# Router work of four batches moved between the items of the top-64 attention

## Chip, cores and metric

One core of one Trainium2 chip runs the kernel. The metric is the device time of one execution in microseconds; lower is better. TensorE does matmuls and transposes, VectorE (DVE) reductions, selections and small tables, ScalarE (ACT) activations and copies out of PSUM, GpSimd (POOL) elementwise work on SBUF and the indirect transfers, SyncE (SP) issues the other transfers.

## What is computed

Four blocks of gated attention and feed-forward over `x` (8 batches, 256 rows, 256 features). The change touches the third block: the top-64 attention and the router of the mixture of experts behind it.

```python
x = x + tanh(g_xattn[2]) * _L2_xattn_ref(_layernorm(x), ctx, ctx, mask, 64, ...)   # 16 heads, 77 keys, best 64 of them
x = x + tanh(g_ffn[2]) * _L2_ffn_ref(_layernorm(x), router_w, w1, w2)

# _L2_ffn_ref: 8 experts, each row goes to the best 2
logits = x_flat @ router_w.T
probs = softmax(logits); top_v, top_i = top_k(probs, 2)
...                       # rows get a place in their experts' lists, in order, up to a capacity
h = gelu(einsum('ech,ehf->ecf', expert_in, w1)); y = einsum('ecf,efh->ech', h, w2)
```

## The kernel before

All activations stay in SBUF as `x[128, 16, 256]`: batch b is rows 2b and 2b + 1 of the middle axis. Each engine runs its own instruction list, written out by hand; the order in the code is the order on the engine. Engines meet in counting semaphores: `then_inc` on the producer and `wait_ge` on the consumer, `past(n)` standing for the n-th count of a phase. A wait blocks everything behind it on that engine.

**The top-64 attention** works on B = 8 batches in PAIRS = 4 pairs, and on each pair in ITEMS = 8 items (4 head groups by 2 batches); N4 = 32 items in all, item i in buffer i % 2. All engines loop over k and handle, in iteration k, items near k:
- TensorE: `top_scores(k + 2)`; a part of the output projection `top_final` if k is in `top_parts`; `top_probs(k - 2)`, eight transposes of probabilities into `ps[2]`; `top_values(k - 2)`; turn and queries of the next pair.
- ScalarE: `top_abs(k - 1)`, `top_out(k - 3)` for every other couple of items, `top_scores(k + 1)` (copy out of PSUM), `top_exp(k - 1)` in two halves of four activations, between them turn and queries of the next pair, `top_turned_probs(k - 2)`, `top_norm` of the next pair.
- GpSimd: `top_shift(k - 1)` with its pads, `top_norm(k - 2)`, `top_mask(k + 1)`, `top_bias` at j = k % 8 in (4, 5), `top_scale` and `top_keys` of the next pair.
- VectorE: `drop_least(k)`, which removes the 13 least of 77 scores of each row and head (a min, then twice max8 and match_replace over 8 rows of 77), then `top_stats`, or `top_residual`, which adds a finished part of the projection to `x`.

`top_parts` sets when the projection of pair q is made: for q = 0, 1, 2 at k = 8q + 10, 14, 15, 16, a quarter each. The rows of pair 0 are complete behind iteration 16, those of pair 1 behind 24. The last pair's projection stands behind the last values: `top_final(3, m)` for m = 0 to 3, m = 0, 1 reading `oT[0]` (which is `xkeep` rows 8 to 11) and m = 2, 3 reading `oT[1]` (rows 12 to 15). `top_last(p)` adds it to `x`.

**The router** works by batch: `l5_stats` (VectorE: mean and variance of two rows), `l5_scale` (GpSimd: the reciprocal root and the shift), `l5_norm` (ScalarE, writes `xkeep`), `l5_flip` (TensorE: four transposes into bank 2), `l5_turned` (ScalarE: copy into `xnT`), `l5_logits` (TensorE: eight matmuls of eight columns into bank 3), and on VectorE `l5_take`, `l5_choose`, `l5_keep`: copy the logits, the best two and their numbers. Behind the last batch VectorE builds the routing tables (cumulative sums, one-hot tiles), GpSimd gathers rows by them, and 39 tiles of 128 rows go through the experts.

**Transfers around it.** SyncE has issued the first weights of all experts and the second of expert 0. It then waits for `done[4]` (all rows of the attention), issues the second weights of experts 1 to 4 (1 MB each), stores of the eight normalised batches (256 KB each, each waiting for its `l5_norm`), the second weights of experts 5 to 7, and, when all stores have landed, the last block's weights.

Of the kernel before, what the change touches and what calls it, by code (L numbers as in the profile page):

```python
# [14 lines left out]
P = 128  # L15
# [11 lines left out]
E = 8  # L27
# [12 lines left out]
def build(nc, a, out, phases=8):  # L40
# [10 lines left out]
    with ctx:  # L51
# [219 lines left out]
        NORMS = (0, 4, 5)  # L271
# [13 lines left out]
        stat = shared("stat", {0: B, 4: TT, 5: B})  # L285
# [3 lines left out]
        xts = shared("xts", {n: B for n in NORMS})  # L289
        done = shared("done", {0: B, 3: TT, 4: TT})  # L290
# [96 lines left out]

        def top_kb(q, p):

            return kb[p] if q else kb_first[p]  # L390
# [11 lines left out]
        def _(sp):  # L402
# [28 lines left out]
            if phases >= 6:  # L431
# [10 lines left out]
                for e in range(E):  # L442
                    first(e)
                second(0)
                sp.wait_ge(done[4].sem, done[4].past(TT))
                for e in range(1, 5):
                    second(e)
                for b in range(B):
                    sp.wait_ge(keep_s.sem, keep_s.past(b + 1))
                    sp.dma_start(xs_d[b * S:(b + 1) * S, :].rearrange("(t p) d -> p t d", p=P),  # L450
                                 xkeep[:, TB * b:TB * b + TB, :]).then_inc(s_kd, 16)
# [25 lines left out]
        def _(gp):  # L477
# [89 lines left out]
            if phases >= 4:  # L567
# [101 lines left out]
                for k in range(N4 + 2):  # L669
# [77 lines left out]
        def _(ac):  # L747
# [205 lines left out]
            if phases >= 4:  # L953
# [12 lines left out]
                def l5_norm(b):  # L966
                    p = b % 2
                    ac.wait_ge(rstd[5].sem, rstd[5].past(b + 1))
                    if b >= B // 2:
                        ac.wait_ge(f_p[4].sem, f_p[4].past(TT))  # L970
                    post_norm(xkeep[:, TB * b:TB * b + TB, :], rows2(b), rs_b[p], nm_b[p]).then_inc(keep_s.sem, 1)

                def l5_turned(b):
# [3 lines left out]
                    copy(xnT[b % 2][:, :, :].rearrange("p c s -> p (c s)"), bank(2)).then_inc(xts[5].sem, 1)  # L977

# [9 lines left out]
                def top_queries(q, p):  # L988
# [104 lines left out]
                for k in range(N4 + 3):  # L1093
# [20 lines left out]
                    if k == N4:  # L1114
                        l5_norm(0)
            if phases >= 5:
                for b in range(1, B):
# [124 lines left out]
        def _(ve):  # L1242
# [237 lines left out]
            if phases >= 4:  # L1480
# [66 lines left out]
                def l5_take(b):  # L1547
                    ve.wait_ge(lg_p.sem, lg_p.past(b + 1))
                    nc.vector.tensor_copy(lg[b % 2][:, :, :], bank(3)[:, 0:TB * E].rearrange("p (t e) -> p t e", t=TB)
# [13 lines left out]
                def l5_keep(b):  # L1563
# [3 lines left out]
                    nc.vector.tensor_copy(topi[:, TB * b:TB * b + TB, :], ix[p][:, :, 0:2]).then_inc(rt_c.sem, 1)  # L1567

# [1056 lines left out]
```

## Time and profile before

| what | us |
| --- | --- |
| median of 3 runs | 994.3 |
| lowest and highest | 991.7, 994.53 |
| profiled execution, its own time | 991.3 |
| its span in the profile | 989.4 |
| items 0 to 31 of the top-64 attention end (last match_replace) | 517.2 |
| last logits of the router taken | 550.9 |
| first expert weights copied | 573.7 |

The last three lines are positions in the span. Line numbers (L...) are those of the kernel before. In a row of the timeline the numbers are start and duration in us, then engine, line, operation, output and inputs, and the idle time of the engine just before with what ended it. An entry `x8` merges eight instructions.

### The profile page before, as it was taken

To read this page: it belongs to the slowest core of one execution; us is meant where nothing else is said; L and a number is where in the kernel's file an instruction comes from. 1 tells how busy PE (TensorE), PEld (TensorE's weight loads), DVE (VectorE), ACT (ScalarE), POOL (GpSimd) and SP (SyncE) were. 2 spreads that over 40 slices of the span, in tenths; PEclk is the share of its full clock that TensorE was granted. 3 is DMA by queue.
4 is the path that set the end of the run, shared out by engine and by line. 5 is a ranking of instruction groups with operands and counts; after the bars stand their busy time and mean duration, and the time that the engine had idled before them with its cause. 6 is when DMAs were issued, how large, how long until landed. Compare 5 with 4: busy or idle time off the path is not lost.

```text
span 989.4 us, 17402 instructions
## 1 busy us (share of the span) xinstructions
PE 812.4 (82%) x5192; PEld 659.3 (67%) x5198; DVE 646.4 (65%) x2713; ACT 516.3 (52%) x1252; POOL 490.3 (50%) x712
## 2 busy tenths in 40 slices
PE   5899999996764767767568479999999999847986
PEld 4577767873452445545347369999999999736775
DVE  3877766889978999999994742222222222367875
ACT  3777755689964889788776012121121211225652
POOL 2566535676635777777565132222323222138993
PEclk9899999999996767879877579999999999968999
DMA  9100001000000090000003911111101111050001
GB/s 292 35 1 2 2 2 43 1 2 0 2 1 1 31 354 1 1 2 1 1 1 103 338 39 38 33 44 32 44 32 37 39 33 33 21 171 0 24 22 42
DMA packets 32934, 47.02 MB, mean 48 GB/s; under 512 B 3158, under 2 KB 27582, under 8 KB 32843
## 3 DMA queue, kind: packets, MB, share of 16 engines
q1 hardware_dynamic: 29099, 35.69, 10.6%
q0 software_dynamic: 3744, 10.23, 3.3%
q8 instruction: 44, 0.72, 0.3%
q14 instruction: 47, 0.39, 0.1%
HBM read 36.60 MB, written 9.31 MB: 46 GB/s over the span
## 4 chain that ended last, share of the span: by engine, by line
PE 52%; DVE 29%; POOL 8%; ACT 4%; issue 4%; DMA 2%; SPq 0%; DVEq 0%; POOLq 0%; ACTq 0%
PE ps L2425 14%; PE ps L2436 14%; DVE experts L1516 5%; DVE experts L1526 5%; DVE m8b L1521 3%; PE ps L1991 3%; DVE m L1511 3%; PE ps L2014 3%; PE ps L1978 2%; DVE mx L1506 2%; PE ps L2001 2%; PE ps L1938 2%; DVE sm L1444 1%; PE ps L2112 1%; DMA x<-in_x 1%
## 5 line engine op out<-in xcount | busy, mean ns | idle before, releaser
L2425 PE MATMUL ps<-xnT,ptall 128*128 128x128 f32 x1248 | 147.3, 277 | 0.0
L2425 PEld LDWEIGHTS ps<-xnT,ptall 128*128 128x128 f32 x1248 | 144.1, 194 | 0.1
L2436 PE MATMUL ps<-experts,wk 128*128 x624 | 141.2, 379 | 1.3 <-ACT xkeep L754 1.3
L1743 DVE COPY ptall<-experts 128x512 f32 x156 | 60.0, 427 | 120.9 <-PE ps L2425 115.1
L699 POOL DMA_INDIRECT xn<-expert_in,rown x39 | 38.1, 976 | 179.2 <-PE ps L2413 164.8
L2436 PEld LDWEIGHTS ps<-experts,wk 128*128 128x128 f32 x624 | 115.6, 190 | 15.8 <-issue 1.7
L1131 ACT ACTIVATE wk<-ps 128x1024 f32<-128x1024 f32 x39 | 39.9, 1024 | 127.4 <-PE ps L2425 127.4
L1028 ACT ACTIVATE experts<-experts,mcol 128x77 f32<-128x77 f32 x256 | 87.8, 350 | 0.1
L754 ACT ACTIVATE xkeep<-ps 128x256 f32<-128x256 f32 x87 | 33.2, 381 | 100.8 <-PE ps L2436 97.1
L1762 DVE COPY xnT<-ps 128x256 f32<-128x256 f32 x39 | 16.5, 424 | 79.0 <-PE ps L2413 79.0
L2280 PE MATMUL ps<-ptall,experts 77*32 77x256 f32 x256 | 25.3, 474 | 51.7 <-ACT ptall L1036 51.7
L523 POOL TENSOR_TENSOR experts<-experts,rden 128x616 f32<-128x616 f32 x32 | 38.8, 1216 | 47.8 <-DVE rden L1301 47.8
L707 POOL DMA_INDIRECT token_out<-xkeep,dest x39 | 38.5, 987 | 44.2 <-ACT xkeep L754 34.1
L613 POOL TENSOR_TENSOR experts<-experts,mx 128x616 f32<-128x616 f32 x32 | 39.1, 1223 | 38.9 <-DVE experts L1526 38.9
L606 POOL TENSOR_TENSOR experts<-experts 128x616 f32<-128x616 f32 x32 | 44.4, 1388 | 26.6 <-ACT experts L1006 26.6
L1516 DVE MATCH_REPLACE8 experts<-m,experts 128x80 f32<-128x80 f32 x256 | 54.7, 233 | 0.0
L1526 DVE MATCH_REPLACE8 experts<-m8b,experts 128x80 f32<-128x80 f32 x256 | 54.7, 233 | 0.0
L2269 PEld LDWEIGHTS ps<-ident,experts 128*77 128x77 f32 x256 | 37.8, 185 | 22.0 <-POOL experts L639 14.2
L2269 PE MATMUL ps<-ident,experts 128*77 128x128 f32 x256 | 43.7, 327 | 10.6 <-POOL experts L639 7.0
L754 ACT ACTIVATE experts<-ps 128x512 f32<-128x512 f32 (+2 forms) x56 | 39.5, 712 | 24.2 <-PE ps L1938 19.0
L754 ACT ACTIVATE ptall<-ps 77x512 f32<-77x512 f32 (+1 forms) x80 | 41.0, 545 | 21.2 <-PE ps L1991 18.2
L1028 ACT ACTIVATION_READ_ACCUMULATOR experts<-experts,mcol 128x1 f32 x256 | 49.3, 193 | 0.0
(303 smaller groups left out, 2049.0 us busy)
## 6 DMA issues: line engine op xcount, KB each, us to landing
experts<-in_ew SPq DMA_DIRECT2D x16, 1024.0 KB, 11.5
experts<-token_out SPq DMA_DIRECT2D x16, 256.0 KB, 5.2
x<-in_x SPq DMA_DIRECT2D x1, 2048.0 KB, 11.0
xkeep<-in_bw SPq DMA_DIRECT2D x2, 1024.0 KB, 7.1
expert_in<-xkeep SPq DMA_DIRECT2D x8, 256.0 KB, 6.5
out<-x SPq DMA_DIRECT2D x8, 256.0 KB, 2.1
xn<-expert_in,rown POOLq DMA_INDIRECT x39, 2.8
token_out<-xkeep,dest POOLq DMA_INDIRECT x39, 2.4
```

Of the source, the lines that this page charges most:

```text
L523: nc.gpsimd.tensor_tensor(flat(soft[j]), flat(soft[j]), rden[i % 2][:, :].unsqueeze(2) .broadcast_to([P, 8, KEYS]), ALU.mult).then_inc(sm_ ...
L606: nc.gpsimd.tensor_tensor(dv, dv, mrow[:, b * KEYS:(b + 1) * KEYS].unsqueeze(1) .broadcast_to([P, TB * HG, KEYS]), ALU.add).then_inc(mk_s, 1)
L613: nc.gpsimd.tensor_tensor(dv, dv, mx[u][:, :].unsqueeze(2).broadcast_to([P, TB * HG, KEYS]), ALU.subtract).then_inc(sc_d.sem, 1)
L754: return nc.scalar.activation(dst, src, ACT.Copy)
L1028: ins = nc.scalar.activation(row, row, ACT.Exp, scale=mcol[:, b:b + 1], accum_out=ssum[u][:, j:j + 1])
L1131: nc.scalar.activation(hidT[j % 2].rearrange("p (v n) -> p v n", v=2), ps[j % 2][:, :, :], ACT.Gelu).then_inc(m_g.sem, 1)
L1516: ins = nc.vector.match_replace(d[j], m8[u][:, j, :], d[j], -BIG)
L1526: ins = nc.vector.match_replace(d[j], m8b[u][:, j, :], d[j], -BIG)
L1743: ins = nc.vector.tensor_copy(tilew[:, v, c, :], experts[:, bass.ds(e * EW + (c * FF + v * 512), 512)])
L2269: ins = nc.tensor.transpose(ps[2][0:KEYS, h // 2, at:at + P], pr[i % 2][:, t, h * KEYS:(h + 1) * KEYS], ident[:, :])
L2425: ins = nc.tensor.matmul(ps[j % 2][:, v, k * P:(k + 1) * P], tilew[:, v, c, k * P:(k + 1) * P], xTb[j % 3][:, c, :], start=c == 0, stop=c ...
L2436: ins = nc.tensor.matmul(bank(4)[:, 0:D], hidT[j % 2][:, k * P:(k + 1) * P], experts[:, bass.ds(e * EW + (E * EW + k * D), D)], start=k == ...
```

## The change

- **Norms and turns.** `l5_at = {16: 0, 20: 1, 24: 2, 28: 3}` puts the router's batches 0 to 3 into the attention loop. For k in it, `l5_stats` follows item k on VectorE; `l5_scale` follows in GpSimd's iteration k + 1 and `l5_norm` in ScalarE's; `l5_flip_half` (four transposes into the upper halves of banks 6 and 7) follows `top_probs` in TensorE's iteration k + 2; `l5_turned_half` (two copies of 128x256 into free halves of `wk[0]`) stands between the exponentials in ScalarE's iteration k + 3.
- **Logits.** `l5_logits_half` of batches 0, 1, 2 stands ahead of the scores of items 23, 27, 31, that of batch 3 in iteration 32; they go to columns 320 to 383 of bank 3. `top_queries(3, 0)` on ScalarE waits for the first of them, because the turned batch 0 lies in its output.
- **Choices.** `l5_pick` (take, keep of the batch before, choose) of batches 0 and 1 stands in VectorE's iteration 32, of 2 and 3 ahead of `top_last`.
- **Last pair's projection.** `top_final(3, 0)` stands ahead of the last values, `top_final(3, 1)` behind them, then 2 and 3. `l5_norm(4)` and `(5)` wait for the first two parts of it instead of all.
- **Behind.** Only batches 4 to 7 are left, with the functions of before.
- **Stores.** Those of batches 0 to 3 stand ahead of the wait for `done[4]`.
- **Semaphores.** `stat`, `rstd`, `xtp` and `xts` of the router become semaphores of their own.

```diff
-        stat = shared("stat", {0: B, 4: TT, 5: B})
+        stat = shared("stat", {0: B, 4: TT})
+        stat[5], rstd[5], xtp[5], xts[5] = (counted(n) for n in ("stat5", "rstd5", "xtp5", "xts5"))
+        l5_at = {16: 0, 20: 1, 24: 2, 28: 3}
+        l5_logit_at = {23: 0, 27: 1, 31: 2}
...
 SyncE
                 second(0)
+                for b in range(B // 2):
+                    stored(b)
                 sp.wait_ge(done[4].sem, done[4].past(TT))
                 for e in range(1, 5):
                     second(e)
-                for b in range(B):
+                for b in range(B // 2, B):
...
 GpSimd
+                    if k - 1 in l5_at:
+                        l5_scale(l5_at[k - 1])
                     if k == N4:
-                        l5_scale(0)
+                        l5_scale(B // 2)
...
 ScalarE
-                        ac.wait_ge(f_p[4].sem, f_p[4].past(TT))
+                        ac.wait_ge(f_p[4].sem, f_p[4].past(TT - 2 if b < B - 2 else TT))
+                def l5_turned_half(b, k):
+                    ac.wait_ge(xtp[5].sem, xtp[5].past(b + 1))
+                    ac.wait_ge(pv_p[4].sem, pv_p[4].past(k - 2))
+                    if b:
+                        ac.wait_ge(lg_p.sem, lg_p.past(b))
+                    for t in range(TB):
+                        ins = copy(xT5[b][:, t, :, :].rearrange("p c s -> p (c s)"), bank(6 + t)[:, S:2 * S])
+                    ins.then_inc(xts[5].sem, 1)
+                    elif q == 3 and p == 0:
+                        ac.wait_ge(lg_p.sem, lg_p.past(1))
+                    if k - 3 in l5_at:
+                        l5_turned_half(l5_at[k - 3], k)
                     if 1 <= k < N4 + 1:
                         top_exp(k - 1, 1)
                     if 2 <= k < N4 + 2:
                         top_turned_probs(k - 2)
+                    if k - 1 in l5_at:
+                        l5_norm(l5_at[k - 1])
...
 VectorE
+                def l5_pick(b):
+                    l5_take(b)
+                    if b:
+                        l5_keep(b - 1)
+                    l5_choose(b)
                     if k == N4:
-                        for b in range(2):
-                            l5_stats(b)
+                        l5_stats(B // 2)
...
+                    if k in l5_at:
+                        l5_stats(l5_at[k])
+                    if k == N4:
+                        for b in range(2):
+                            l5_pick(b)
-                for b in range(2, 5):
-                    l5_stats(b)
+                l5_stats(B // 2 + 1)
+                for b in range(2, B // 2):
+                    l5_pick(b)
                 for p in range(2):
                     top_last(p)
+                    l5_stats(B - 2 + p)
...
 TensorE
+                def l5_flip_half(b, k):
+                    pe.wait_ge(keep_s.sem, keep_s.past(b + 1))
+                    pe.wait_ge(oc_s, sum(i // 2 % 2 for i in range(k - 2)))
+                    for t in range(TB):
+                        for c in range(CH):
+                            ins = nc.tensor.transpose(bank(6 + t)[:, S + c * P:S + (c + 1) * P],
+                                                      xkeep[:, TB * b + t, c * P:(c + 1) * P], ident[:, :])
+                    ins.then_inc(xtp[5].sem, 1)
+                def l5_logits_half(b):
+                    pe.wait_ge(xts[5].sem, xts[5].past(b + 1))
+                    ...
+                            ins = nc.tensor.matmul(l5_cols(b)[:, t * E:(t + 1) * E], xT5[b][:, t, c, :], rwT[:, c, :],
+                                                   start=c == 0, stop=c == CH - 1)
+                    ins.then_inc(lg_p.sem, 1)
+                    if i in l5_logit_at:
+                        l5_logits_half(l5_logit_at[i])
...
+                    if k == N4:
+                        pe.wait_ge(sc_r[4].sem, sc_r[4].past(N4))
+                        pe.wait_ge(done[4].sem, done[4].past(top_parts[k - 2] + 1))
+                        l5_logits_half(B // 2 - 1)
                     if 2 <= k < N4 + 2:
                         top_probs(k - 2)
+                        if k - 2 in l5_at:
+                            l5_flip_half(l5_at[k - 2], k)
+                        if k - 3 in l5_at:
+                            pe.wait_ge(xts[5].sem, xts[5].past(l5_at[k - 3] + 1))
                         if k == N4 + 1:
-                            l5_flip(0)
+                            top_final(PAIRS - 1, 0, k)
                         top_values(k - 2)
                     if k >= N4 + 2:
-                        for m in range(2 * (k - N4 - 2), 2 * (k - N4 - 1)):
+                        for m in range(1, 2) if k == N4 + 2 else range(2, 4):
                             top_final(PAIRS - 1, m, k)
-                for b in range(1, B):
+                l5_flip(B // 2)
+                for b in range(B // 2 + 1, B):
                     l5_flip(b)
                     l5_logits(b - 1)
```

## Rows read from the trace of the kernel before

**Rows 1.** The page: VectorE's busy share in 40 slices of the span, tenths.
```profile
DVE  3877766889978999999994742222222222367875
```
**Rows 2.** Busy time by stretch: from:to, length, engines' busy us, clock, DMA share, GB/s.
```profile
411.50:517.20 105.70, 72.36 (x392) 49.48 (x392) 105.70 (x809) 85.49 (x321) 71.03 (x76) 0.80 0.00 1
497.50:504.00 6.50, 4.34 (x20) 2.52 (x20) 6.50 (x52) 5.20 (x21) 4.95 (x5) 0.74 0.00 1
510.80:517.20 6.40, 4.54 (x25) 3.47 (x24) 6.40 (x52) 5.20 (x19) 2.16 (x2) 0.59 0.00 0
517.20:535.30 18.10, 14.70 (x95) 11.85 (x95) 7.01 (x28) 10.41 (x30) 10.75 (x23) 0.72 0.00 1
535.30:551.10 15.80, 14.83 (x84) 14.00 (x83) 8.26 (x76) 8.51 (x17) 4.29 (x12) 0.65 0.98 317
551.10:573.70 22.60, 4.85 (x36) 3.25 (x36) 18.64 (x55) 0.22 (x1) 3.86 (x2) 0.50 0.77 261
```
**Rows 3.** The chain of waits in order of time, 517 to 552: start, length.
```profile
528.36 6.06 PE ps L2314 x32
...
549.04 1.86 PE ps L2299 x8
```
**Rows 4.** Timeline of VectorE: start and duration in us.
```profile
503.94 0.80 DVE L1506 TENSOR_REDUCE mx<-experts 128x8 f32<-128x616 f32 x1
...
517.68 0.71 DVE L1539 BATCH_NORM_STATS2 st_b<-x 128x6 f32<-128x256 f32 x2
...
518.53 0.72 DVE L1539 BATCH_NORM_STATS2 st_b<-x 128x6 f32<-128x256 f32 x2
```
**Rows 5.** Timeline of GpSimd, from k = 16 to the drain.
```profile
418.39 1.22 POOL L613 TENSOR_TENSOR experts<-experts,mx 128x616 f32<-128x616 f32 x1
...
500.59 1.28 POOL L606 TENSOR_TENSOR experts<-experts 128x616 f32<-128x616 f32 x1 [0.46 <-ACT experts L1006]
501.82 1.27 POOL L632 TENSOR_TENSOR x<-x,experts 128x512 f32<-128x512 f32 x1
...
519.84 0.23 POOL L590 TENSOR_SCALAR rs_b<-mv_b 128x2 f32<-128x2 f32 x1
...
520.96 0.50 POOL L595 TENSOR_SCALAR nm_b<-mv_b,rs_b 128x1 f32<-128x1 f32 x2
```
**Rows 6.** Who waited for whom, 411.5 to 517.2: total us, times, longest.
```profile
PE ps L2280 <- ACT ptall L1036: 26.3, 15, 3.3
```
**Rows 7.** Timeline of ScalarE.
```profile
503.13 1.01 ACT L1036 ACTIVATE ptall<-ps 77x1024 f32<-77x1024 f32 x1
505.37 0.72 ACT L1017 ACTIVATE experts<-experts 128x616 f32<-128x616 f32 x1 [1.23 <-POOL experts L613]
...
528.71 1.08 ACT L772 ACTIVATE xkeep<-x,nm_b,rs_b 128x256 f32<-128x256 f32 x2
```
**Rows 8.** Timeline of TensorE.
```profile
500.19 1.99 PE L2269 MATMUL ps<-ident,experts 128*77 128x128 f32 x8
...
517.56 0.64 PE L2280 MATMUL ps<-ptall,experts 77*32 77x256 f32 x8 [1.11 <-ACT ptall L1036]
518.13 1.16 PE L2314 MATMUL ps<-experts,xkeep 128*128 128x128 f32 x8
519.80 1.10 PE L2269 MATMUL ps<-ident,experts 128*77 128x128 f32 x8 [0.52 <-POOL experts L639]
...
534.24 0.60 PE L1938 MATMUL ps<-ident,xkeep 128*128 128x128 f32 x4
534.68 0.96 PE L2299 MATMUL ps<-rwT,xnT 128*128 128x8 f32 x8
...
541.18 1.09 PE L1938 MATMUL ps<-ident,xkeep 128*128 128x128 f32 x4
542.06 1.71 PE L2299 MATMUL ps<-rwT,xnT 128*128 128x8 f32 x8
```
**Rows 9.** Busy time in stretches of 2 us, columns as in rows 2.
```profile
522.00:524.00 2.00, 0.83 (x8) 0.20 (x8) 1.67 (x7) 2.00 (x5) 1.38 (x2) 0.71 0.00 0
...
532.00:534.00 2.00, 2.00 (x15) 2.00 (x14) 0.75 (x1) 0.00 (x0) 1.15 (x3) 0.73 0.00 0
...
540.00:542.00 2.00, 2.00 (x11) 2.00 (x11) 0.86 (x10) 1.06 (x3) 1.43 (x4) 0.50 1.09 361
```

More of the change, by code:

```diff
@@ L270, in build @@
         SC = B * GR
-        NORMS = (0, 4, 5)
+        NORMS = (0, 4)
         s_x = sem("s_x")
@@ L386, in build, with l5_cols @@
         top_parts = {ITEMS * q + 10 + (0, 4, 5, 6)[m]: 4 * q + m for q in range(PAIRS - 1) for m in range(4)}
+        l5_at = {16: 0, 20: 1, 24: 2, 28: 3}
+        l5_logit_at = {23: 0, 27: 1, 31: 2}
+        xT5 = [wk[0][:, CH * h:CH * h + CH, :].rearrange("p c s -> p (c s)").rearrange("p (t c s) -> p t c s", t=TB, c=CH)
+               for h in (1, 0, 0, 0)]
+        def l5_cols(b):
+            return bank(3)[:, 320 + TB * E * b:320 + TB * E * (b + 1)] if b < B // 2 else bank(3)[:, 0:TB * E]
         def top_kb(q, p):
@@ L1111, in _ @@
                         top_turned_probs(k - 2)
+                    if k - 1 in l5_at:
+                        l5_norm(l5_at[k - 1])
                     if k // ITEMS + 1 < PAIRS and k % ITEMS in (1, 2):
                         top_norm(k // ITEMS + 1, k % ITEMS - 1)
-                    if k == N4:
-                        l5_norm(0)
             if phases >= 5:
-                for b in range(1, B):
+                l5_norm(B // 2)
+                for b in range(B // 2 + 1, B):
                     l5_norm(b)
@@ L1643, in _ @@
                         top_residual(top_parts[k] // 4, top_parts[k] % 4, k)
-                for b in range(2, 5):
-                    l5_stats(b)
+                    if k in l5_at:
[6 more added lines that the diff above has]
+                    l5_pick(b)
                 for p in range(2):
                     top_last(p)
+                    l5_stats(B - 2 + p)
             if phases >= 5:
-                for b in range(B):
-                    if b + 5 < B:
-                        l5_stats(b + 5)
-                    l5_take(b)
-                    if b:
-                        l5_keep(b - 1)
-                    l5_choose(b)
+                for b in range(B // 2, B):
+                    l5_pick(b)
                 l5_keep(B - 1)
@@ L2237, in top_queries @@
                     ins.then_inc(q_p[4].sem, 1)
+                def l5_flip_half(b, k):
[8 more added lines that the diff above has]
+                    pe.wait_ge(xts[5].sem, xts[5].past(b + 1))
+                    if b == 0:
+                        pe.wait_ge(s_w[5], 16)
+                    for t in range(TB):
+                        for c in range(CH):
+                            ins = nc.tensor.matmul(l5_cols(b)[:, t * E:(t + 1) * E], xT5[b][:, t, c, :], rwT[:, c, :],
+                                                   start=c == 0, stop=c == CH - 1)
+                    ins.then_inc(lg_p.sem, 1)
                 def top_scores(i):
@@ L2383, in _ @@
                     if k >= N4 + 2:
-                        for m in range(2 * (k - N4 - 2), 2 * (k - N4 - 1)):
+                        for m in range(1, 2) if k == N4 + 2 else range(2, 4):
                             top_final(PAIRS - 1, m, k)
             if phases >= 5:
-                pe.wait_ge(s_w[5], 16)
-                for b in range(1, B):
+                l5_flip(B // 2)
+                for b in range(B // 2 + 1, B):
                     l5_flip(b)
```

12 lines of the change are left out of this document (7 added, 5 removed).

## The prediction

> **What bounds the kernel now.** I read the page first: VectorE's row is at nine tenths or more through the top-64 attention and falls off right behind it [rows 1]. Then the busy time by stage [rows 2]. From 411.5 to 517.2 us VectorE has no idle time at all (105.70 of 105.70 us); TensorE is busy for 72 us, ScalarE for 85, GpSimd for 71. From 517.2 to 551.1 the picture turns: VectorE is busy for 15 of 34 us, and TensorE for 29.5. From 551.1 to 573.7 VectorE works off the routing tables alone (18.6 of 22.6 us). So an edit costs in the attention what it adds to VectorE, and gains behind 517.2 what it takes from a chain that passes through TensorE. The chain of waits shows that chain in order [rows 3]: the last item's shift on GpSimd, its exponentials, turn and values, 32 matmuls of the last pair's projection (528.36, 6.06 us), the last residual on VectorE, then the router's batches on TensorE up to the last logits (549.04, 1.86 us). The routing tables start when those are in, at 550.93.
>
> **What the change adds to the attention.** It puts `l5_stats` of batches 0 to 3 on VectorE behind items 16, 20, 24 and 28. One `l5_stats` is two bn_stats and two bn_aggr: it starts at 517.68, the next at 518.53 [rows 4], so 0.85 us. VectorE has no idle time there, so all of it lies on the path: 4 x 0.85 = **+3.4 us**. Before, the first five lay in VectorE's idle time behind 517.57 and the others beside TensorE's work, so taking them away there gives nothing by itself.
>
> The other engines have room, and I take their additions at nothing; here is the cover. One item takes VectorE 6.43 us (its reduction starts at 497.52, that of the next item at 503.94, which is the row shown) [rows 4]. What must be ready for an item is GpSimd's mask, which started at 500.59 and took 1.28 us, until 501.87, for the reduction at 503.94 [rows 4, 5]: 2.07 us of cover in a typical item.
> - GpSimd gets one `l5_scale` each at k = 17, 21, 25, 29: 0.23 + 0.71 + 0.50 us with gaps, 519.84 to 521.46, so 1.65 us [rows 5]. At k = 21 and 29 it stands behind `top_bias` (1.27 us, 501.82 to 503.09) [rows 5]: from the shift at 497.69 to there it is 5.4 us, and 7.05 with the new part, in an iteration that the new statistics have made 6.43 + 0.85 = 7.28 us long. It fits. The trace has a like case: at k = 16 two `top_scale` ran in one iteration, the next shift followed them at 418.39 without a gap [rows 5], and VectorE was still never idle.
> - ScalarE gets a norm (two pieces, 528.71 to about 529.7, 1.05 us) in the same iterations and a turn copy (two pieces of 0.36 us, about 0.65) at k = 19, 23, 27, 31. At 505.37 it had waited 1.23 us for GpSimd's shift [rows 7]. 1.05 us against 1.23 + 0.85: hidden. At k = 17 `top_norm` of pair 3 is queued behind it and at k = 21 and 22 the queries of pair 3: a delay of up to 1.3 us there, if `top_queries(3, 0)` has to wait for the first logits, is still under 2.07.
> - TensorE gets four transposes at k = 18, 22, 26, 30, and eight logit matmuls ahead of the scores at k = 21, 25, 29: 0.60 and 0.96 us at the fast clock, 1.09 and 1.71 at the slow one [rows 8]. The transposes stand where it waits for ScalarE's turned probabilities anyway (26.3 us in 15 waits) [rows 6]. The logits delay the scores and the probabilities' transposes; the latter end at 502.18 for a copy at 503.13 [rows 7, 8], so 0.95 us are free and up to 0.8 us reaches ScalarE, again under 2.07.
> - SyncE stores batches 0 to 3 (4 x 256 KB) before it waits for `done[4]`. Nothing else is queued there but the weights that wait for the same semaphore, so this costs nothing and takes 1.05 MB out of the stretch behind.
>
> If the cover were gone, each norm iteration would cost VectorE up to 1.65 + 1.05 = 2.7 us: the upper bound is 4 x 2.7 = 10.8 us.
>
> A rule of the Trainium skill speaks against this (SBUF — State Buffer, section "Who interferes with whom"): a VectorE instruction with two inputs in SBUF and a GpSimd instruction that reads SBUF take the same read interface, and the later one blocks. By it the four added `l5_scale` could hold VectorE for up to 4 x 1.65 = 6.6 us. The trace does not bear it out for the selection's instructions: an item lasted 6.5 us with GpSimd busy for 4.95 us, and 6.4 us with 2.16 [rows 2], with the same 52 instructions. I take nothing.
>
> **The drain, 517.2 to the end of the projection.** All in times of before; the shift of 3.4 us comes on top. Logits of batch 3 (about 1 us) go ahead of the projection part at 518.13 and of the transposes at 519.80 [rows 8]; these have until 522.12, when ScalarE is through its exponentials, so nothing. VectorE has `l5_stats(4)`, a residual that is 1 us later, and two `l5_pick` (0.75 and 0.85 us: the take at 536.04, the next at 537.65 with statistics between). It comes to the last reciprocal at 522.45 instead of 522.24, and the norm behind it still ends before TensorE is free at 524.25. So nothing until the last item's probabilities are turned at 526.2. Then `top_final(3, 0)` stands in the gap in which ScalarE copies them (until 527.28) instead of the flip of batch 0. At the slow clock eight of its matmuls take 2.05 us (32 took 6.11 us over both clocks), so values start at 528.0 instead of 527.28 and end at 529.0; final 1 ends at 531.0, final 2 at about 532.6, final 3 at 533.7 by the clock of before. Before, the last ended at 534.24: **-0.5 us**. The wait of `l5_norm(4)` for `TT - 2` lets norms 4 and 5 run from 531.0, beside the last two finals.
>
> **The router.** Before, from 534.24 to the last take at 550.93: 16.7 us for seven flips and eight groups of logits, at 1.6 us a batch at the fast clock (0.60 for the flip and 0.96 for the logits) and 2.45 at the slow one (1.09 and 1.71, partly over each other: flips at 541.18, 543.63, 546.08) [rows 8]. Now four batches are left. At the fast clock the path is the last batch's, through four engines: residual 0.8 us, statistics 0.85, scale 1.65, norm 1.05, turn of batch 6 0.6, flip of 7 0.65, its copy and logits 6 1.0, take and logits 7 1.3: 8.0 us. At the slow clock TensorE sets it: 4 x 2.45 = 9.8 and 1.5 for the first turn and last take, 11.3 us. Which clock? It rose between 532 and 534, when TensorE had been busy without a gap of more than 0.3 us since 524.2, and fell at 540, 5.3 us into the router [rows 9]. I take the same here: fast until 539, slow for the last three groups, 9.3 us. So **-16.7 + 9.3 = -7.4 us**.
>
> **Behind it.** The tables, 550.93 to 573.7, keep their work. The weights must have landed by 573.7: their transfers began with `done[4]` at 535.3 and ran at about 360 GB/s [rows 9]; in the table stage they fill 0.77 of 22.6 us where a full stretch shows 1.09, so 16 us, until 567 [rows 2, 9]. That is 10.9 MB with stores and the last block's weights. Now they start 0.75 us earlier, and 7.3 MB of weights and 1.05 MB of stores take 23.3 us: until 559.6, with the first use at 566.3. It stays hidden with over 6 us to spare; uncovered it costs what it is late. In the expert tiles nothing changes.
>
> **The sum.** 3.4 - 0.5 - 7.4 = **-4.5 us**, so 991.3 becomes 986.8 us for the profiled execution. The four executions shown lie at 991.3, 991.7, 994.3 and 994.5; by the median, 994.3 becomes 989.8. I say **989.5**.
>
> **The rivals.**
> 1. The fast clock holds through drain and router (16%). For it: the added matmuls fill the gaps at 518 to 520, and at 522 to 524 the clock of before was on its way down (0.71) [rows 9]. Transposes then take 1.1 us instead of 1.99, values 0.64 instead of 1.08, finals 1.1: the projection ends at 530.1, the router 8.0 us later, at 538.1. 550.9 to 538.1 is -12.8, with 3.4 it is -9.4: 984.9 us.
> 2. The slow clock holds through both (12%). For it: eight-column logits ran at 0.50 from 540 on though TensorE was busy all the time. Finals end at 535.2, the router at 546.5: -4.4 + 3.4 = -1.0, 993.3 us, no measurable change.
> 3. VectorE stalls in the attention (14%): at k = 17, 21, 25, 29 ScalarE's norm waits for GpSimd's scale, with the next item's abs and scores queued behind it, so the mask is late. Against it: 2.07 us of cover and 0.85 of lengthening. At the bound of 10.8 us it gives 994.3 - 4.5 + 10.8 = 1000.6 us, slower. It cancels the gain at 1.1 us per norm iteration and decides for slower from 1.9 us (7.5 us in all). I give each half of the 14%.
> 4. The skill's read-interface rule holds (3%): up to 6.6 us more, 996.4 us; two thirds of it within no change.
> 5. The transfers become the last wait (3%): only if stores and weights run 6 us longer than their rate gives; then no change.
>
> My forecast has 52%. A measurement of this kernel can tell about 0.3%, 3 us. Faster: 52 + 16 = 68%. Same: 12 + 7 + 2 + 3 = 24%. Slower: 7 + 1 = 8%. The range goes from rival 1 (984.9) to rival 2 (993.3), rounded up to 994 for small stalls.
>
> **What would show it.** In the profile after: four pairs of bn_stats between items with no idle time of VectorE up to the last item (else rival 3), which ends at 520.6 instead of 517.2; 8 final matmuls ahead of the last values; four flips and four logit groups behind the finals, 8 to 11 us; the granted clock from 520 to 550 tells the forecast from rivals 1 and 2; the table stage 22.6 us long, with no wait for the weights at its end. The forecast is wrong if the last item ends later than 522, or if the table stage grows.

## The result and the profile after

The changed kernel takes 986.87 us (median of 8 runs, 985.06 to 988.4), the kernel before 990.71 (8 runs, 989.1 to 994.53). The ratio is 0.9941, with a 95% interval of 0.9922 to 0.996: faster by 0.4 to 0.8%. The profiled execution has a span of 986.0 us against 989.4.

The stretches of the span of the changed kernel, cut at events close to the cuts of [rows 2]: start of item 16's first reduction, end of item 31, start of the last residual of the last projection, start of the last take of logits, start of the first copy of weights. Columns: from:to, length, busy us of TensorE, its weight loads, VectorE, ScalarE, GpSimd, granted clock, DMA share, GB/s.

```profile
413.98:523.09 109.11, 75.88 (x436) 52.49 (x440) 109.11 (x825) 91.69 (x337) 76.86 (x92) 0.81 0.03 11
523.09:536.91 13.82, 12.39 (x91) 10.27 (x84) 7.81 (x52) 8.16 (x25) 6.47 (x11) 0.77 0.01 2
536.91:547.62 10.71, 8.66 (x48) 8.23 (x45) 4.22 (x33) 4.70 (x9) 2.86 (x8) 0.63 0.85 272
547.62:570.38 22.76, 4.86 (x36) 3.25 (x36) 18.80 (x54) 0.22 (x1) 3.86 (x2) 0.50 0.92 305
```

VectorE has no idle time in the first, as before. In the kernel before the same cuts give 17.22 us for the drain, which is the stretch from the end of item 31 to the last residual (517.28 to 534.50), 16.43 for the router (to 550.93) and 22.77 for the tables. From the first reduction of item 16 to that of item 31 it is 99.16 us before and 102.59 now. So the changes are +3.4 us in the items, -3.4 in the drain, -5.7 in the router and 0.0 in the tables, in all -5.7 us from item 16 to the first weights. The span shows only -3.4 because this execution reached item 16 2.4 us later than the profiled one of before (413.98 against 411.60), in stages that the change does not touch.

The four additions show as pieces of VectorE's timeline, for batch 0:

```profile
420.41 0.48 DVE L1611 SCALAR_TENSOR_TENSOR x<-ps,gates,x 128x256 f32<-128x256 f32 x1
420.80 0.74 DVE L1570 BATCH_NORM_STATS2 st_b<-x 128x6 f32<-128x256 f32 x2
421.46 0.30 DVE L1575 BATCH_NORM_AGGREGATE mv_b<-st_b 128x2 f32<-128x6 f32 x2
421.68 0.78 DVE L1537 TENSOR_REDUCE mx<-experts 128x8 f32<-128x616 f32 x1
```

From 420.80 to 421.68 it is 0.88 us. The item after it, which has `l5_scale(0)` beside it on GpSimd (425.41), takes 6.41 us; before it took 6.43.

TensorE in the drain and the router after, to be read against [rows 8]:

```profile
531.09 1.10 PE L2328 MATMUL ps<-ident,experts 128*77 128x128 f32 x8
532.03 1.06 PE L2373 MATMUL ps<-experts,xkeep 128*128 128x128 f32 x8
533.30 0.64 PE L2339 MATMUL ps<-ptall,experts 77*32 77x256 f32 x8 [0.22 <-ACT ptall L1064]
533.87 2.94 PE L2373 MATMUL ps<-experts,xkeep 128*128 128x128 f32 x24
536.65 0.60 PE L1976 MATMUL ps<-ident,xkeep 128*128 128x128 f32 x4
538.03 0.63 PE L1976 MATMUL ps<-ident,xkeep 128*128 128x128 f32 x4 [0.78 <-ACT xnT L771]
538.49 0.96 PE L2358 MATMUL ps<-rwT,xnT 128*128 128x8 f32 x8
540.32 1.09 PE L1976 MATMUL ps<-ident,xkeep 128*128 128x128 f32 x4 [0.87 <-ACT xnT L771]
541.20 1.72 PE L2358 MATMUL ps<-rwT,xnT 128*128 128x8 f32 x8
```

The first part of the last projection stands at 532.03 in the gap ahead of the values, and the other 24 matmuls take 2.94 us, 0.12 each. In the kernel before, the flip of batch 0 filled that gap to 0.26 us, and the 32 matmuls behind it took 6.11 us, 0.19 each; these are its rows and its clock:

```profile
525.96 1.06 PE L1938 MATMUL ps<-ident,xkeep 128*128 128x128 f32 x4
527.28 1.08 PE L2280 MATMUL ps<-ptall,experts 77*32 77x256 f32 x8 [0.26 <-ACT ptall L1036]
528.29 6.11 PE L2314 MATMUL ps<-experts,xkeep 128*128 128x128 f32 x32
```

```profile
522.00:523.00 1.00, 0.00 (x0) 0.00 (x0) 0.76 (x4) 1.00 (x3) 0.47 (x1) 0.93 0.00 0
...
533.00:534.00 1.00, 1.00 (x10) 1.00 (x10) 0.00 (x0) 0.00 (x0) 0.25 (x2) 0.95 0.00 0
```

The clock of the changed kernel in stretches of 2 us, against [rows 9]:

```profile
524.00:526.00 2.00, 2.00 (x10) 2.00 (x11) 0.41 (x3) 1.55 (x6) 1.83 (x4) 0.50 0.04 8
530.00:532.00 2.00, 1.55 (x16) 1.07 (x17) 1.97 (x18) 0.68 (x2) 1.83 (x3) 1.00 0.01 4
...
538.00:540.00 2.00, 1.42 (x12) 1.36 (x12) 1.14 (x10) 1.39 (x3) 1.57 (x5) 0.94 0.43 97
540.00:542.00 2.00, 1.68 (x9) 1.71 (x9) 0.35 (x4) 1.77 (x4) 0.37 (x2) 0.50 1.03 359
```

So the clock is up from 529.6 to 539.8, with the whole last projection in it. In the kernel before it was down from 522.9 to 533.1, and came up when more than half of the projection was done.

### The profile page after: what moved, and what is told of

The parts are those of the page before. It is cut to its first block, busy times and chain, and to the rows that moved or that the text cites. A ratio compares the mean times of both kernels' runs of the same rounds, so it can differ in the third digit from the quotient of the medians.

```text
span 986.0 us, 17413 instructions
## 1 busy us (share of the span) xinstructions
PE 810.2 (82%) x5192; PEld 657.3 (67%) x5198; DVE 647.0 (66%) x2713; ACT 516.3 (52%) x1256; POOL 491.0 (50%) x712
## 4 chain that ended last, share of the span: by engine, by line
PE 52%; DVE 28%; POOL 9%; issue 5%; ACT 5%; DMA 2%; SPq 0%; DVEq 0%; POOLq 0%; ACTq 0%
PE ps L2492 14%; PE ps L2503 14%; DVE experts L1547 5%; DVE experts L1557 4%; PE ps L2029 3%; DVE m8b L1552 3%; DVE m L1542 3%; PE ps L2052 3%; PE ps L2016 3%; DVE mx L1537 2%; PE ps L2039 2%; PE ps L1976 2%; DVE sm L1475 1%; PE ps L2150 1%; DMA x<-in_x 1%
## 5 line engine op out<-in xcount | busy, mean ns | idle before, releaser
L2503 PEld LDWEIGHTS ps<-experts,wk 128*128 128x128 f32 x624 | 115.6, 190 | 15.8 <-issue 1.7
```

The source lines that it names most:

```text
L2503: ins = nc.tensor.matmul(bank(4)[:, 0:D], hidT[j % 2][:, k * P:(k + 1) * P], experts[:, bass.ds(e * EW + (E * EW + k * D), D)], start=k == ...
```

## The experiments

Two questions were open. One is whether the drain's 3.4 us is the work of the split (the first part of the last projection ahead of the last values) or luck of the clock. The other is what the attention's and the router's parts are worth. The table has the stretches of all kernels in us, one profile each, cut as above. "To item 16" and "last block" (from the last store of an expert tile to the end) hold no instructions that differ between the kernels but the raising of four semaphores at the start. "First tile" goes from the first weight copy to the first tile's store.

| kernel | to item 16 | items 16 to 31 | drain | router | tables | first tile | last block | median of runs |
| --- | --- | --- | --- | --- | --- | --- | --- | --- |
| before | 411.60 | 99.16 | 17.22 | 16.43 | 22.77 | 18.33 | 125.4 | 990.71 |
| before_again | 412.45 | 99.13 | 17.22 | 16.42 | 22.76 | 18.33 | 125.6 | 992.47 (one) |
| changed | 413.98 | 102.59 | 13.82 | 10.71 | 22.76 | 18.30 | 125.4 | 986.87 |
| again | 413.62 | 102.61 | 12.34 | 10.70 | 22.78 | 18.30 | 125.2 | 986.67 |
| no_stats | 411.64 | 99.84 | 13.07 | 9.40 | 22.76 | 18.79 | 125.8 | 984.98 |
| final_old | 414.23 | 102.59 | 17.74 | 9.56 | 22.77 | 18.61 | 125.6 | 990.71 |
| stores_late | 413.94 | 102.60 | 13.81 | 10.71 | 22.76 | 18.31 | 125.7 | 988.09 |
| gap_filled | 412.93 | 102.60 | 14.55 | 9.50 | 22.76 | 18.68 | 125.6 | 987.38 |
| split_only | 414.27 | 99.14 | 13.67 | 15.59 | 22.77 | 18.95 | 126.2 | 991.67 |
| warm_tables | 413.63 | 102.60 | 12.34 | 10.71 | 22.77 | 16.72 | 126.6 | 986.71 |
| busy_router | 413.82 | 102.63 | 13.83 | 8.06 | 22.77 | 19.60 | 126.4 | 987.31 |
| norm_all | 413.36 | 102.82 | 14.65 | 12.19 | 22.76 | 19.31 | 126.1 | 991.46 |
| both_busy | 415.00 | 102.60 | 12.33 | 8.06 | 22.68 | 16.81 | 126.2 | 984.57 |
| all_busy | 413.42 | 102.61 | 13.61 | 8.07 | 22.76 | 16.72 | 125.8 | 983.80 |

The 38 tiles between the first and the last store take 271.9 us in every one of them. The untouched columns move by 3.4 and 1.4 us from execution to execution, so a difference of less than 2 us is to be read from the stretches, not from the whole.

The runs were taken in four sets, each beside runs of the kernel before, whose median was 990.71 us in the set of the result, 991.19 in that of again, no_stats, final_old and stores_late, 994.3 in that of gap_filled, split_only, warm_tables and busy_router, and 992.04 in that of norm_all, both_busy and all_busy. A difference of medians from two sets can therefore be off by up to 3.6 us. Each ratio below is to the kernel before in the same set.

**The kernels again.** No edit.

> The changed kernel once more, beside the kernel before on the same chip. Theory A (the three terms: statistics +3.5 us on VectorE, drain -3.4, router -5.7, together -5.6): a ratio of about 0.994 to 0.995. Theory B (3 us of the first comparison were chance, the drain being shorter only because the granted clock happened to be high in it): about 0.9975. The profile tells how long the drain is when the clock falls at another place: by A 13.9 us from the last residual of the items to that of the projection, by B up to 17.

986.67 us against 991.19, ratio 0.9954 (0.9937 to 0.9971), which leaves theory B's 0.9975 out. The drain was 12.3 us this time: the clock was down from 524.3 to 527.7, where it had been down from 522.7 to 529.6. Over all profiles with the split the drain lies between 12.3 and 14.7 us; without it, and with nothing else in its place, it was 17.2 in both profiles of before and 17.7 in final_old.

> The kernel before, profiled a second time. If the length of its drain is a matter of the granted clock's chance, it lies anywhere between 12.3 and 17.7 us; if the gap of 0.3 us and the low clock ahead of the last values are its habit, 17 to 18 us again, and 16 to 17 us of router behind it.

Drain 17.22 and router 16.42 once more; the long drain is the habit of the order before. Theory A stands, theory B falls.

**The statistics.** Left out for batches 0 to 3:

```diff
-                        l5_stats(l5_at[k])
+                        ve.wait_ge(done[4].sem, done[4].past(TB * l5_at[k] + TB))
+                        ve.sem_inc(stat[5].sem, 1)
```

> Leaves out the statistics of batches 0 to 3, so that their norms use what lies in the buffers and their routing is not the reference's. If VectorE is the only bound in the attention, each item behind 16, 20, 24 and 28 is 0.87 us shorter and the whole 3.5 us faster than the changed kernel (983.4). Rival: the iterations that hold a norm, a scale and logits were carried by the 0.87 us that the statistics add, and without them ScalarE or GpSimd is late: idle time of VectorE ahead of its reductions, and a gain of 1 us or less.

The kernel leaves these statistics out, so the norms of batches 0 to 3 use what lies in the buffers; it is there for its time alone. The items take 99.84 us, 2.8 less than with the statistics and 0.7 more than before. The waits of VectorE in the items show where the 0.7 is:

```profile
DVE rden L1529 <- ACT experts L1056: 0.6, 1, 0.6
```

Once, VectorE waits 0.6 us for ScalarE's exponentials. So of the 3.4 us that the items grew by, 2.8 come back without the statistics; the cover that the other engines need for norms, turns and logits is there, but 0.7 us short without the time that the statistics themselves add. The median, 984.98, is 1.7 us under the changed kernel, half of what was expected.

**The projection.** As before, all four parts behind the last values:

```diff
-                        if k == N4 + 1:
-                            top_final(PAIRS - 1, 0, k)
-                        for m in range(1, 2) if k == N4 + 2 else range(2, 4):
+                        for m in range(2 * (k - N4 - 2), 2 * (k - N4 - 1)):
```

> The changed kernel with the last pair's projection as before: all four parts behind the last values. If the split is what shortened the drain, the projection ends one part later, 1.1 us at the fast clock or 2.05 at the slow one, less the 0.2 us that the values wait: +0.9 to +1.8 us (988 to 989). If the shorter drain is the clock's doing: within 0.5 us of the changed kernel.

990.71 us, ratio to before 0.9989 (0.9972 to 1.0007): 4 us more than with the split (986.67 in the same set), and without the split the rest of the change cannot be told from no change. Both expectations, +0.9 to +1.8 us and within 0.5, were too low. The timeline of TensorE shows why:

```profile
531.34 1.10 PE L2328 MATMUL ps<-ident,experts 128*77 128x128 f32 x8
533.55 1.08 PE L2339 MATMUL ps<-ptall,experts 77*32 77x256 f32 x8 [1.11 <-ACT ptall L1064]
534.56 6.41 PE L2373 MATMUL ps<-experts,xkeep 128*128 128x128 f32 x32
```

```profile
532.00:534.00 2.00, 0.89 (x13) 0.41 (x10) 0.72 (x9) 1.02 (x1) 0.89 (x3) 0.79 0.00 0
534.00:536.00 2.00, 2.00 (x14) 1.44 (x7) 0.00 (x0) 0.38 (x1) 0.00 (x0) 0.50 0.00 0
```

TensorE is idle for 1.11 us while ScalarE copies the last probabilities, as it had been ahead of the values at 530.60; the clock goes from 1.00 to 0.50 in that second gap (0.79 over the first of these stretches) and stays down until 540, for 5.4 of the projection's 6.4 us. To see whether order or occupation counts, the gap was filled with two matmuls that nobody reads, and all four parts left behind the values:

```diff
+                        if k == N4 + 1:
+                            for _ in range(2):
+                                nc.tensor.matmul(bank(0)[:, 0:256], ident[:, :], x[:, 0, :], start=True, stop=True)
```

> The changed kernel with all four parts of the projection behind the last values, as in final_old, and two matmuls of 128x256 whose result nobody reads in the place of the part that stood ahead of them. Theory C (the split gains by keeping TensorE occupied while ScalarE copies, so that the granted clock stays up through the 24 or 32 matmuls behind it): those 32 take about 4 us instead of 6.4, the drain is about 1 us longer than in the changed kernel, the whole near 987.7. Theory D (the split gains by its order, work done earlier): as final_old, 990.7.

```profile
530.81 1.03 PE L2444 MATMUL ps<-x,ident 128*128 128x256 f32 x4
532.08 0.64 PE L2339 MATMUL ps<-ptall,experts 77*32 77x256 f32 x8 [0.24 <-ACT ptall L1064]
532.65 3.84 PE L2373 MATMUL ps<-experts,xkeep 128*128 128x128 f32 x32
```

32 matmuls in 3.84 us, the drain 14.55, the whole 987.38 (ratio to before 0.9936, 0.9911 to 0.9962). Of the 3.9 us of drain between final_old and the changed kernel 3.2 come back with no useful work moved; the 0.7 that are left are what the order gives. Theory C stands for the changed kernel. The Trainium skill (TensorE: Matmul & The Clock Gate, section "HAM oscillation — how this bites in real kernels") says that idle gaps between bursts of matmuls bring the clock down and that the next burst then starts slow. This pair of kernels agrees in the direction; the gaps in the Trainium skill's example are much longer waits for transfers, and here 1.11 us between two short bursts went with the fall.

This explains why the clock stays up once it is up. It doesn't explain when it comes up. Counted from the end of item 31, it rose after 15.8 us in both profiles of before, though the flip of batch 0 filled the gap there, but after 6.5 us in the changed kernel and also in final_old. Here are final_old and split_only (below, 9.5 us):

```profile
523.00:529.00 6.00, 6.00 (x31) 5.19 (x32) 2.77 (x18) 3.57 (x17) 3.82 (x6) 0.50 0.01 3
530.00:533.00 3.00, 1.74 (x16) 1.03 (x16) 2.69 (x22) 1.45 (x3) 2.64 (x5) 1.00 0.01 3
```

```profile
523.00:529.00 6.00, 4.55 (x25) 3.37 (x24) 2.56 (x11) 4.28 (x17) 4.39 (x10) 0.50 0.01 3
530.00:543.00 13.00, 11.84 (x103) 10.69 (x102) 7.96 (x58) 10.08 (x21) 7.14 (x20) 1.00 0.58 187
```

So the drain's -3.4 us are a chain of three steps: +0.5 for everything but the split (before to final_old), -3.2 for the clock held by work in the gap (to gap_filled), -0.7 for the order (to the changed kernel). The last three can be set side by side, since their clock fell within 0.4 us of the end of item 31 and rose 6.5 to 6.8 us behind it. Why the clock rises that much earlier in all three kernels than in the kernel before is open. And it isn't always so: in norm_all, whose code is that of the changed kernel up to the norms, it was down from 523.3 to 533.5, and the drain was still only 14.65.

**The split by itself**, in the kernel before, with the flip of batch 0 moved behind the last part:

```diff
                         if k == N4 + 1:
-                            l5_flip(0)
+                            top_final(PAIRS - 1, 0, k)
                         top_values(k - 2)
...
+                        if k == N4 + 3:
+                            l5_flip(0)
```

> The kernel before with the split alone: the first part of the projection ahead of the last values, the flip of batch 0 moved behind the last part; no router work in the attention. Theory C: the gap ahead of the last values was nearly filled by that flip already and the clock was low there, so the split gives at most its 0.5 us and loses about 1 for the flip: 990.5 to 992. Theory E (the split alone carries the whole gain of the change): about 987 to 988.

991.67 us, ratio 0.9991 (0.9969 to 1.0013). The ratio shows no gain, though the medians of the set differ by 2.6 us (991.67 and 994.3). The stretches show one: the drain is 13.67 instead of 17.22 and the router 15.59 instead of 16.43, together -4.4 us. In this profile 2.7 of them are taken back in a column that the split does not touch (to item 16), 0.6 in the first tile and 0.8 in the last block. So the 0.5 us that were expected at most of the split in the old kernel were too few: the clock rose 9.5 us behind the end of item 31 instead of 15.8. The whole cannot carry a verdict on theory E. From item 16 to the first store the split alone gives -3.8 us, the moved router work alone (final_old) -2.6, the change -5.7 and -7.2 (again).

**The stores**, all eight behind the wait for the attention:

> The changed kernel with all eight stores behind the wait for all rows of the attention, as before. If the transfers have room (they ended 4 us ahead of the first weight copy, by the DMA share of the stretches), 1.05 MB at 360 GB/s, 2.9 us, is hidden: no change within 0.5 us. Rival: the gathers and the last block's weights then overlap and the first tile is late by up to 2.9 us.

Every stretch up to the last store is that of the changed kernel to 0.1 us, and the last block is 0.3 longer. The median, 988.09 (ratio 0.9963, 0.9946 to 0.9981), is 1.4 us above that of again in the same set, where 0.5 at most was expected. The stretches agree with hidden stores; the two ratios' intervals overlap, so the 1.4 us are not shown to be more than what varies. The transfers of the changed kernel end between 566 and 568 us, ahead of the first weights at 570.38:

```profile
564.00:566.00 2.00, 1.29 (x16) 0.92 (x15) 2.00 (x2) 0.00 (x0) 0.00 (x0) 0.50 1.10 379
566.00:568.00 2.00, 0.70 (x8) 0.52 (x8) 1.07 (x7) 0.00 (x0) 0.00 (x0) 0.50 0.37 133
```

**The earlier norms**: `l5_norm` waiting for all parts.

```diff
-                        ac.wait_ge(f_p[4].sem, f_p[4].past(TT - 2 if b < B - 2 else TT))
+                        ac.wait_ge(f_p[4].sem, f_p[4].past(TT))
```

> The changed kernel with the wait of l5_norm(4) and (5) as before: for all four parts of the last projection. At the fast clock the last two parts take under 2 us, so the two norms (2.08 us together) start about 1.8 us later; the router's path passes through the scale of batch 6 at about the same time, so I expect 0.5 to 1.5 us more in the router and 987.5 to 988.5. Rival: they are hidden behind the statistics and scale of batch 6: within 0.3 us.

991.46 us, ratio to before 0.9989 (0.9971 to 1.0006). By the ratios that is 3.5 to 4.8 us more than the changed kernel (0.9954 and 0.9941), where 0.5 to 1.5 were expected. Its timeline of ScalarE, and then that of the changed kernel:

```profile
537.33 2.08 ACT L789 ACTIVATE xkeep<-x,nm_b,rs_b 128x256 f32<-128x256 f32 x4 [2.52 <-PE ps L2373]
539.31 0.58 ACT L771 ACTIVATE xnT<-ps 128x512 f32<-128x512 f32 x1
540.23 1.09 ACT L789 ACTIVATE xkeep<-x,nm_b,rs_b 128x256 f32<-128x256 f32 x2 [0.34 <-POOL nm_b L610]
```

```profile
535.12 2.08 ACT L789 ACTIVATE xkeep<-x,nm_b,rs_b 128x256 f32<-128x256 f32 x4 [0.74 <-PE ps L2373]
537.29 0.60 ACT L771 ACTIVATE xnT<-ps 128x512 f32<-128x512 f32 x1
538.61 1.09 ACT L789 ACTIVATE xkeep<-x,nm_b,rs_b 128x256 f32<-128x256 f32 x2 [0.72 <-POOL nm_b L610]
```

The norms start with the end of the last part instead of 1.7 us ahead of it, and TensorE waits 1.25 us for them, so the router is 12.19 us long, 1.5 more. The other 2 to 3 us are not all explained: the drain (+0.8), the first tile (+1.0) and the last block (+0.7) were longer in the profile. In the two former the clock differs: it stayed down from 523.3 to 533.5, and in the first tile it rose 9.0 us behind the first weight copy instead of 7.0. I can't say from one profile whether it did so in all 12 runs.

**The clock of the tables and of the router.** Unread matmuls behind the one-hot tiles, and, by themselves, in the router:

```diff
+                for _ in range(7):
+                    nc.tensor.matmul(bank(7)[:, 0:256], ident[:, :], x[:, 0, :], start=True, stop=True)
             if phases >= 6:
                 pe.wait_ge(routed.sem, routed.past(1))
```

> The changed kernel with seven matmuls of 128x256 that nobody reads behind the one-hot tiles, while VectorE finishes the tables and nothing else needs TensorE. The clock is at 0.50 from the router on until 3 us into the first expert tile. If it rises by them ahead of the tile, the tile's first 32 matmuls take 3.6 us instead of 5.2 and the whole is 1.5 to 2.5 us faster than the changed kernel (984.5). Rival: the clock does not rise on these few, or they delay the first tile: no change or up to 0.5 us slower.

```diff
                 l5_flip(B // 2)
+                keep_busy(2)
                 for b in range(B // 2 + 1, B):
                     l5_flip(b)
                     l5_logits(b - 1)
+                    if b == B // 2 + 1:
+                        keep_busy(2)
```

> The changed kernel with two unread matmuls of 128x256 behind the first flip of the router and two behind its first logits, where TensorE waits for ScalarE. If the clock falls at 538 to 540 for want of work on TensorE, it holds longer, and the last three batches take 1.6 instead of 2.45 us each: the router 8.0 to 9.5 us instead of 10.7, 1 to 2.5 us faster. Rival: they delay flip and logits by their own 0.9 us a pair and the clock falls anyway: 0.5 to 1 us slower.

warm_tables: the first tile's first 32 matmuls take 3.74 us, those of the kernel again 5.12, and the first tile is 1.6 us shorter:

```profile
564.84 5.21 PE L2472 MATMUL ps<-x,ident 128*128 128x256 f32 x14
...
572.37 3.74 PE L2494 MATMUL ps<-xnT,ptall 128*128 128x128 f32 x32
```

```profile
572.57 5.12 PE L2492 MATMUL ps<-xnT,ptall 128*128 128x128 f32 x32
```

busy_router: the clock stays up to the last logits, and the router takes 8.06 us instead of 10.71, to 0.1 us the 8.0 that the prediction gave for four batches at the fast clock (its terms add up to 7.9):

```profile
542.00:544.00 2.00, 1.64 (x15) 1.58 (x15) 1.01 (x12) 0.60 (x1) 0.00 (x0) 1.00 1.09 372
544.00:546.00 2.00, 0.79 (x8) 0.70 (x7) 1.38 (x15) 0.00 (x0) 0.00 (x0) 1.00 1.10 350
```

But its first tile takes 1.3 us longer (19.60), because the clock rises 9.7 us behind the first weight copy instead of 7.0. In both medians (986.71, 987.31; ratios 0.9933, 0.9908 to 0.9957, and 0.994, 0.9919 to 0.9961) no gain over the changed kernel shows, and both missed what was expected. The last block was about 1 us longer in both profiles. Together:

> The changed kernel with the unread matmuls of warm_tables and of busy_router together. Each alone shortened its own stretch (first tile 1.6 us earlier; router 8.1 instead of 10.7) and showed no change in the whole. If both gains are real and the whole was blurred by the stretches ahead and by the last block: router 8.1, first tile 1.6 us earlier, 983 to 984.5. If they are given back behind, in the last block: 986.5, with the last block 1 to 2 us longer than 125.4.

984.57 us (6 runs, 984.07 to 986.61; ratio to before 0.9933, 0.9908 to 0.9958), with the router at 8.06 and the first tile at 16.81. The median is 2.3 us under that of the changed kernel, but from another set; the ratio's interval overlaps with that of the changed kernel. So the gain is shown in the two stretches, -2.6 and -1.5 us, and not yet in the whole. With the third group, four unread matmuls in iteration 31:

```diff
+                        if k == N4 - 1:
+                            pe.wait_ge(sc_r[4].sem, sc_r[4].past(N4))
+                            pe.wait_ge(done[4].sem, done[4].past(top_parts[k - 1] + 1))
+                            for _ in range(4):
+                                nc.tensor.matmul(bank(2)[:, 0:256], ident[:, :], x[:, 0, :], start=True, stop=True)
```

> As both_busy, and four more unread matmuls in iteration 31 ahead of the values, where TensorE waits 2.4 us for ScalarE and the clock then falls in the drain. If the clock then holds through logits of batch 3, projection part and transposes, ScalarE no longer waits for the transposes (1.26 us in the changed kernel) and the drain is 12.3 us instead of 13.8: 982 to 983.5. Rival: ScalarE is the drain's bound there already (its exponentials): 12.3 us at best, no different from both_busy in the whole.

983.80 us (6 runs, 983.29 to 986.14), ratio to before 0.9926 (0.9901 to 0.9952). Its median is the lowest of all, but the third group does not do what was expected: the clock holds through logits and projection part and falls at 528 instead, so that the last probabilities are turned slowly and the drain is 13.61, more than the 12.33 of both_busy without that group.

```profile
526.00:528.00 2.00, 0.17 (x2) 0.00 (x0) 1.34 (x13) 2.00 (x11) 0.83 (x4) 1.00 0.00 0
528.00:530.00 2.00, 1.57 (x11) 0.76 (x12) 1.97 (x17) 0.77 (x2) 1.83 (x3) 0.57 0.02 4
```

TensorE did almost nothing from 526 to 528 (0.17 us). The 0.8 us to both_busy are within what varies.

## Why the prediction came out as it did

The sign and the range were right, and so was the term of the attention. What failed is the size, in two steps: the drain's term, costed at the clock of before, and the basis on which the sum was set. The terms of drain and router missed by -2.9 and +1.7 us. That their sum, -4.5, comes near the -5.7 of the stretches is luck, since the two errors mostly cancel.

- **"The sum": "by the median, 994.3 becomes 989.8. I say 989.5".** The -4.5 us were set on the median of three runs, two of which were at 994.3 and 994.5. With five more the median of before is 990.71, so 989.5 states a change of -1.2 us, while -3.8 was measured by the medians and -5.8 by the ratio. The other basis stood in the same paragraph: the profiled execution, 991.3, which gives 986.8. That this meets the measured 986.87 is luck too, since the -4.5 holds the two errors and the profiled execution of the changed kernel took 988.16.
- **"The drain": "by the clock of before ... -0.5 us".** Measured -3.4. The schedule was right in its order: the first part in the gap, values, then the other three. But each was costed at the clock at which TensorE had run there before. In the changed kernel the clock is up again 6.5 us behind the end of item 31 instead of 15.8, and the moved part keeps it up by filling the gap ahead of the last values, so that 24 matmuls follow at 0.12 us each where most had gone at up to 0.26. The second half is shown by final_old and gap_filled: without anything in the gap +3.9 us of drain, with idle work in it +0.7. The first half, why the clock rises earlier, stays open.
- **"The router": -7.4.** Measured -5.7 (16.43 to 10.71), from cuts that differ by 0.3 us. The clock fell at 539.8, which is 2.9 us into the router where 5.3 were taken (in the kernel before it fell at 540.0, 5.5 us into it). The last three groups of logits ran slow, as the prediction has it. What it has no term for is TensorE's idle time ahead of two flips, 0.78 and 0.87 us, in which it waited for ScalarE's copies. With the clock held up, busy_router gives 8.06, the lower of the two bounds.
- **"What the change adds to the attention": +3.4.** Measured 3.43. No idle time of VectorE in the items; rival 3 falls. The lengthening by the statistics is part of the cover: no_stats.
- **The Trainium skill's read-interface rule** (SBUF — State Buffer, "Who interferes with whom"), rival 4: an item with `l5_scale` beside it took 6.41 us, one without 6.43. So nothing is blocked there, but the test is weak: by their rows the reduction, max8 and match_replace of an item read one large operand in SBUF each, and the rule is about instructions with two. Whether it holds for those no run here shows.
- **The transfers**, rival 5, were hidden; stores_late has the same stretches up to the last store. The forecast's 23.3 us were too few, though: they ran from 537.7 to about 567, some 29 us, because that sum leaves out the last block's weights (1.4 MB, issued from 555.9 on). So 3 to 4 us were to spare ahead of 570.38, not over 6.
- **Rivals 1 and 2**, the clock up or down throughout: the drain went as rival 1 has it from 530 on, the router as between the two. Their two ends, -9.4 and -1.0, hold the measured change.
- **The marker "the forecast is wrong if the last item ends later than 522"** was badly chosen: the item ended at 523.09 with every item as long as forecast, since the stages ahead ended 2.4 us later. A length would have been the marker, not a position.

Open: why the clock rises earlier behind item 31 in the changed kernel; why norm_all costs 3.5 to 4.8 us by its ratio where its stretches show 1.5 by the wait; and whether the last block's 1 us in warm_tables and busy_router is chance. For chance speaks that split_only and norm_all, without unread matmuls, show 126.2 and 126.1 as well, and all_busy, with the most of them, 125.8.

## What to carry to other kernels

Cost a moved matmul with the clock that the moved order leaves behind it: a gap of 1.1 us just ahead of the last values and a burst of 32 matmuls cost 3.2 us here, which unread work in the gap gave back. Filling a gap is no guarantee: in the kernel before it was filled and the clock was low all the same. Where VectorE alone bounds a stage, what is added there is paid in full (3.4 us) even when all that it feeds is free; it was worth it only because the router behind it was 5.7 us shorter. And state a forecast against the runs' whole spread: the four executions known then lay in two pairs 2.6 us apart, and 29 later runs of the same kernel filled 988.3 to 995.7, so the choice of the basis weighed as much as the sum.

## What was not expected of the hardware

- The drain of one kernel was 13.82 us in an execution whose clock came up at 529.6, and 12.34 in one where it came up at 527.7. The stretch to item 16, which the change does not touch, moved by 3.4 us between profiles; its mean clock doesn't order it (0.91 with 411.60 in before, 0.92 with 414.27 in split_only), so the cause is open. Meanwhile 38 tiles of steady matmuls took 271.9 us in each of 14 profiles.
- Each semaphore that ScalarE raises at the start costs it time ahead of its first instruction: its table load stood at 4.70 to 4.71 us in the three profiles with the old set, and at 5.29 in the eleven with four more semaphores, 0.15 us each. First row the kernel before, second the changed one. It shows no effect behind: TensorE's first matmul waited for a transfer in both, until 7.98 and 7.30 us.

```profile
4.71 1.28 ACT L757 ACT_TABLE_LOAD   x1 [4.71 <-issue]
```

```profile
5.29 1.28 ACT L774 ACT_TABLE_LOAD   x1 [5.29 <-issue]
```
